# A decoder kernel: context spectra and keys moved into the first attention, correlation in two halves, accumulating transposes, a full last chunk

## The chip, the cores and the metric

The kernel runs on one core of one Trainium2 chip, as one program. The metric is its device time in microseconds (us). PE is the engine of matrix products (TensorE), DVE is VectorE, ACT is ScalarE, POOL is GpSimd, and SP (SyncE) issues the transfers. A chip core has on-chip memory (SBUF) and eight PSUM banks, into which PE writes.

## The reference, cut to what matters

A decoder of four layers; each layer adds an attention, a cross attention with a context and a feed-forward part to x, of 8 x 256 tokens and 256 features. Four parts matter here.

```python
# layer 0, attention: for each head h, q, k, v = 16x16 products of layernorm(x)
probs = softmax((q * k).sum(-1) / 16, axis=batch); x += probs * v.sum(over t)
# layer 0, cross attention: 16 heads of 16 features
q = layernorm(x) @ Wq.T + bq;  k, v = ctx @ Wk.T + bk, ctx @ Wv.T + bv
corr = irfft(rfft(q, t) * conj(rfft(k, t))).mean(head's features)
w, delays = top_k(corr, 5);  w = softmax(w)
x += (sum over delays of w * v shifted by delay) @ Wo.T + bo
# layer 0, feed-forward: mixture of 8 experts, two per token, 704 hidden features
y = (silu(z @ gate.T) * (z @ up.T)) @ down.T
# layer 3, attention: causal, with relative positions
att = q @ k.T + take_along(rel_pos_emb @ k.T, distance);  y = softmax(att / 4) @ v
```

## The kernel before, in words

Work is tiled in 16 tiles of 128 tokens (two a batch element), in four groups of four tiles for the norms. Each stage of the decoder is a class with one method per engine; the method writes that engine's instructions in their order, so each engine runs its own list, stage after stage, and waits only on counters (`wait_ge`). Nothing else orders the work. `Uses` deals out PSUM banks: `take` makes PE wait until the bank's last use has been emptied by the engine that was named for it, `fills` and `empties` raise the counters. All arithmetic that matters here is in float32. `products` (L218 to L222) is the helper that writes an accumulating product, so most of PE's records bear line 221; `copied` (L225 to L239) takes a bank out on ACT or DVE (L230, L234).

**Start (`begin`, L3336).** SP issues x, tables, the first stage's weights, the Fourier table and its inverse, and at the end two stores of zeros (2 MB each) for a result buffer of the second mixture (L3363). Norms of the four groups of x are begun by DVE (L253, L256), POOL (L263 to L271), z is written by DVE (L274: two tiles of a group) and ACT (L330: the other two), and PE turns z (L404), with copies out at L230 and L234.

**First attention (`L0Attention`, L616).** PE multiplies turned z by a 128x128 matrix, pair of tiles by pair (L651, eight pairs `qz`), and DVE multiplies the result with z (L681). Then DVE sums it by head over the 4096 columns (L684) and sums z over time (L687), takes a softmax across the batch (L693 to L698) and scales the values, which PE spreads over the partitions (L658, one bank for each of eight batch elements), adds them to x (L703, L706) and begins the next norm. SP waits for the logits (L694) and then issues the transfers of the next stage: the context (2 MB), four weights and four bias rows.

**Autocorrelation (`L0Autocorrelation`, L720).** PE, all by `spectrum` and `project`, eight banks each: spectra of the context, keys from them, spectra of z (waits for z), queries, values. DVE and ACT take the banks out in turns (`taken_out`), values go by ACT alone. POOL adds a bias to one row of each key, query and value (L923) and forms the fourth product of spectra (L935). DVE, when all queries and keys are in and biased, forms three products of 2048 columns (L872 to L874), sums over heads' features (L875, L876), subtracts (L878) and sums again (L879). PE inverts the result, a chain of short DVE operations picks the best five delays and weighs them (L885 to L900, ACT's exponential L850 in between), PE turns and transforms the weights, DVE and POOL multiply them with the values (L858), and PE inverts and projects. POOL's list has, between the values' biases and that, four additions of the output's bias to x (`Bias.pool`, L452, 1024 columns each).

**First mixture (`L0Mixture`, L1215).** 39 blocks of 128 rows, each with the weights of its expert (2.18 MB by SP from a ring of four). Per block PE does two halves of gate and up (352 columns), turns the 704 hidden features of the block before in six chunks of which the last has 64 (L1291), and multiplies them with `down` (six products of 256 columns, the last with 64 rows). ACT copies chunks 0 to 3 out (L1339), DVE the last two, each by a copy of its own (L1384); ACT takes out the block's result (L1348).

**Attention loop (`Attention`, L1666).** Used in the middle attention (layer 1, 48 units), in a smaller stage, and in the last one (layer 3, 48 units, with positions). A unit has two banks of scores: PE writes the mask (L1734), scores from 32-row tiles (L1738) and, with positions, adds them by products with the identity (L1743: eight blocks of 128x128 a unit); DVE takes the maximum (L1828), ACT the exponentials (L1803), PE turns them (L1754, eight transposes a unit), DVE copies (L1839), PE multiplies with the values (L1769) every other unit.

Of the kernel before, what the change touches and what calls it, by code (L numbers as in the profile page):

```python
# [13 lines left out]
ALU = mybir.AluOpType  # L14
# [3 lines left out]
P = 128  # L18
B, T, D = 8, 256, 256
TILES = B * T // P  # L20
DC = D // P
# [593 lines left out]

class L0Attention(Stage):  # L616


    def __init__(self, k):
# [4 lines left out]
        self.prod = k.slab[0].rearrange("p (i c) -> p i c", i=TILES)  # L624
        self.tmp = k.slab[1][:, 0:1024].rearrange("p (n a h e) -> p n a h e", n=2, a=2, h=H)
        self.fetch = Fetch(k, (self.wq, k.d["L0_attn_Wq"]), (self.wk, k.d["L0_attn_Wk"]), (self.wvT, k.d["L0_attn_WvT"]))
        self.norm = Norm(k)
        u = self.uses = Uses(k)
        self.m_use = u.add("dve")
        self.qz = [u.add("dve") for _ in range(TILES // 2)]  # L630
        self.v = [u.add("dve") for _ in range(B)]
# [6 lines left out]
    def pe(self):  # L638
# [5 lines left out]
        for n, u in enumerate(self.qz):  # L644
# [8 lines left out]
            mm.then_inc(use.fills(u), 1)  # L653
        pe.wait_ge(self.summed)
        for b, u in enumerate(self.v):
            bank = use.take(u)
            for c in range(DC):
                mm = nc.tensor.matmul(bank[:, P * c:P * c + P], self.sumT[:, B * c + b:B * c + b + 1].to_broadcast([P, P]),  # L658
                                      self.wvT, start=True, stop=True)
            mm.then_inc(use.fills(u), 1)  # L660
            if b % 2:
                self.next.norm.pe_final(b // 2)

    def act(self):
        act = self.k.act
        self.norm.act_zT(GROUPS - 1)
        act.wait_ge(self.shifted)
        self.k.nc.scalar.activation(self.s, self.s, ACT.Exp, scale=1.0 / float(D) ** 0.5).then_inc(self.exps.up(), 1)
        for g in range(GROUPS):
            self.next.norm.act_final(g)  # L670

    def dve(self):
# [26 lines left out]
        for b, u in enumerate(self.v):  # L699
            v4 = use.bank(u)[:, 0:D].rearrange("p (h e) -> p h e", h=H).unsqueeze(1).to_broadcast([P, 2, H, HD])  # L700
            p4 = self.s[:, 2 * b:2 * b + 2, :].unsqueeze(3).to_broadcast([P, 2, H, HD])
            dve.wait_ge(*use.filled(u))
            nc.vector.tensor_tensor(self.tmp[:, b % 2], v4, p4, ALU.mult).then_inc(use.empties(u), 1)  # L703
            dve.wait_ge(*use.emptied(u))
# [10 lines left out]
    def sp(self):  # L715
        self.k.sp.wait_ge(self.shifted)
        self.next.fetch.sp()


class L0Autocorrelation(Stage):  # L720


    def __init__(self, k):
        self.k, slab = k, k.slab
        self.ctx = slab[0].rearrange("p (i c) -> p i c", i=TILES)
        self.zfT, self.cfT = (slab[n].rearrange("p (c b f) -> p c b f", c=DC, b=B) for n in (1, 2))
        self.qf, self.kf, self.vf = (slab[n].rearrange("p (a b n) -> p a b n", a=2, b=B) for n in (3, 4, 5))
        self.wq, self.wk, self.wv, self.wo = (weight(slab[6], 512 * n, DC, D) for n in range(4))
# [12 lines left out]
        self.fetch = Fetch(k, (self.ctx, by_tile(d["ctx"])),  # L741
                           *[(w, by_chunk(d["L0_xattn_" + n])) for w, n in
                             ((self.wk, "WkT"), (self.wv, "WvT"), (self.wq, "WqT"), (self.wo, "WoT"))],
                           *[(r, d["L0_xattn_" + n]) for r, n in
                             ((self.bq, "bq"), (self.bk, "bk"), (self.bv, "bv"))],
                           (self.bo, d["L0_xattn_bo"].to_broadcast([P, D])))
# [4 lines left out]
        self.cf = [u.add(turns[b % 2]) for b in range(B)]  # L751
        self.kfs = [u.add(turns[(b + 1) % 2]) for b in range(B)]
        self.zf = [u.add(turns[b % 2]) for b in range(B)]
        self.qfs = [u.add(turns[(b + 1) % 2]) for b in range(B)]
# [6 lines left out]
        self.crossed = k.counter("cross_products", "pool").reserve(1)  # L761
# [7 lines left out]
    def spectrum(self, uses, src, ready):  # L769
        k, use = self.k, self.uses  # L770
        for b, u in enumerate(uses):
            for mark in ready(b):
                k.pe.wait_ge(*mark)
            bank = use.take(u)
            for c in range(DC):
                mm = products(k.nc, bank[:, T * c:T * c + T],
                              [(src[:, 2 * b + a, P * c:P * c + P], k.fourier[:, a, :]) for a in range(2)])
            mm.then_inc(use.fills(u), 1)

    def project(self, uses, src, w, spectra):  # L780
        k, use = self.k, self.uses
        for b, u in enumerate(uses):
            k.pe.wait_ge(*use.emptied(spectra[b]))
            bank = use.take(u)
            for half in range(2):
                mm = products(k.nc, bank[:, D * half:D * half + D],
                              [(src[:, c, b, P * half:P * half + P], w[:, c, :]) for c in range(DC)])
            mm.then_inc(use.fills(u), 1)

    def pe(self):  # L790
        k, nc, pe, use = self.k, self.k.nc, self.k.pe, self.uses
        pe.wait_ge(k.fourier_loaded)
        pe.wait_ge(self.fetch.loaded)
        self.spectrum(self.cf, self.ctx, lambda b: [])
        self.project(self.kfs, self.cfT, self.wk, self.cf)
        self.spectrum(self.zf, k.z, lambda b: self.norm.z_in(2 * b + 1))
        self.project(self.qfs, self.zfT, self.wq, self.zf)
        self.project(self.vfs, self.cfT, self.wv, self.cf)
# [25 lines left out]

    def spectra_out(self, engine, uses, dst, pattern, names):
        k, use = self.k, self.uses
        q = k.dve if engine == "dve" else k.act
        for b, u in enumerate(uses):
            if use.by(u, engine):
                q.wait_ge(*use.filled(u))  # L830
# [2677 lines left out]
```

## Time and profile before

| | |
|---|---|
| median of 3 runs | 2892.08 us (2885.71 to 2893.25) |
| profiled execution | 2892.69 us, span 2891.4 us |
| PE busy | 2459.8 us (85%) |
| DVE busy | 1218.3 us (42%) |
| ACT busy | 876.3 us (30%) |
| POOL busy | 556.1 us (19%) |
| mean granted clock of PE | 0.915 of 2.4 GHz |

Times in the profile are microseconds from the start of the span. A record names line, engine, operation, output from input by name, shape, and how many stand together; a matmul's record lasts longer than the step from one to the next, as they are pipelined, so a group is priced from its start to the next group's start. PEld are weight loads. In brackets stands the idle time before, and who ended it. Activity at which no engine waits for another is read from the groups' starts.

### The profile page before, as it was taken

What the parts mean: (1) busy time and instruction counts of PE and PEld (TensorE: products, weight loads), DVE (VectorE), ACT (ScalarE), POOL (GpSimd) and SP (SyncE); (2) the same over time, 40 slices, a digit from 0 to 9 for tenths busy, and PEclk for the clock granted to TensorE, in tenths of its full rate; (3) what the DMA queues carried; (4) which work ended last, traced back from release to release, by engine and by line L of the source; (5) the groups of instructions that cost most, each with busy time, mean ns of one, the idle gap of its engine ahead of it and who ended that gap; (6) DMA issues with size and microseconds to landing.
All of it is one profiled execution on the core that took longest, in us unless ns stands there. A gap on an engine that the chain in (4) does not pass through costs nothing.

```text
span 2891.4 us, 33874 instructions
## 1 busy us (share of the span) xinstructions
PE 2459.8 (85%) x13454; PEld 1668.8 (58%) x13454; DVE 1218.3 (42%) x2269; ACT 876.3 (30%) x2374; POOL 556.1 (19%) x552
## 2 busy tenths in 40 slices
PE   3965999949996779787999999699957999877999
PEld 3854666626674555223566657577732788633555
DVE  6363121257687472565333312300045455655220
ACT  1211222223673341563222321122214444313220
POOL 1441222224101011211444310233120100012000
PEclk8976999969898889898999998799977999988999
DMA  4004777730001000200000002233129232100000
GB/s 152 1 5 191 281 295 284 291 123 1 2 2 49 1 1 29 92 1 29 1 1 0 1 0 73 64 106 96 43 90 364 117 130 91 38 26 1 8 8 15
DMA packets 75380, 224.17 MB, mean 78 GB/s; under 512 B 9359, under 2 KB 52758, under 8 KB 65239
## 3 DMA queue, kind: packets, MB, share of 16 engines
q1 hardware_dynamic: 67894, 204.76, 19.5%
q0 software_dynamic: 7328, 17.26, 1.7%
q8 instruction: 106, 1.74, 0.2%
q14 instruction: 52, 0.42, 0.0%
HBM read 178.61 MB, written 45.17 MB: 77 GB/s over the span
## 4 chain that ended last, share of the span: by engine, by line
PE 48%; DVE 6%; DMA 2%; ACT 1%; POOL 1%; issue 1%; SPq 0%; POOLq 0%; DVEq 0%; ACTq 0%
PE psum L221 26%; PE psum L3198 6%; PE psum L1743 3%; PE psum L2241 2%; PE psum L3207 2%; PE psum L2228 2%; PE psum L1738 2%; DMA positions<-arena 2%; PE psum L1754 1%; DVE stats L253 1%; PE psum L1769 1%; DVE arena L2288 1%; PE psum L2458 1%; POOL small L2656 1%; PE psum L404 1%
## 5 line engine op out<-in xcount | busy, mean ns | idle before, releaser
L221 PE MATMUL psum<-arena 128*128 128x256 f32 (+6 forms) x4100 | 1060.6, 414 | 25.9 <-DVE arena L3294 12.9
L221 PEld LDWEIGHTS psum<-arena 128*128 128x128 f32 (+2 forms) x4100 | 717.3, 184 | 325.8 <-issue 160.5
L1828 DVE TENSOR_REDUCE small<-psum 128x4 f32<-128x1024 f32 (+1 forms) x112 | 137.0, 1223 | 157.4 <-PE psum L1743 110.9
L263 POOL TENSOR_SCALAR x_moments<-x_moments 128x4 f32<-128x4 f32 x48 | 12.0, 249 | 954.2 <-DVE x_moments L256 953.7
L3198 PE MATMUL psum<-arena 128*128 128x512 bf16 x768 | 166.4, 379 | 0.0
L1176 POOL DMA_INDIRECT l_out<-arena,slot_tables x79 | 78.7, 996 | 456.0 <-ACT arena L1348 255.5
L1803 ACT ACTIVATE arena<-psum,small 128x128 f32<-128x128 f32 (+1 forms) x384 | 148.9, 417 | 48.0 <-DVE small L1828 48.0
L1367 DVE TENSOR_TENSOR arena<-arena,psum 128x352 f32<-128x352 f32 x78 | 40.7, 521 | 265.5 <-ACT arena L1326 265.5
L1839 DVE COPY arena<-psum 128x512 f32<-128x512 f32 x224 | 143.6, 681 | 1.8 <-PE psum L1754 1.5
L1803 ACT ACTIVATE z<-psum,small 128x128 f32<-128x128 f32 (+1 forms) x256 | 103.8, 426 | 119.2 <-DVE small L1828 119.2
L404 PE MATMUL psum<-ident,z 128*128 128x128 f32 x256 | 47.1, 344 | 108.6 <-DVE z L274 79.9
L1738 PE MATMUL psum<-arena 32*128 32x128 f32 (+1 forms) x1280 | 133.2, 339 | 0.0
L3198 PEld LDWEIGHTS psum<-arena 128*128 128x128 bf16 x768 | 75.2, 98 | 90.5
L2656 POOL TENSOR_TENSOR small<-small,minus_half 128x16 f32<-128x16 f32 x32 | 92.8, 2901 | 179.2 <-DVE small L2570 179.2
L221 PE MATMUL psum<-zT,arena 128*128 128x512 f32 x240 | 115.2, 636 | 7.3 <-DVE zT L234 4.7
L2786 ACT ACTIVATE arena<-psum,small 128x269 f32<-128x269 f32 x128 | 61.5, 485 | 185.1 <-PE psum L221 173.6
L330 ACT ACTIVATE z<-x,x_shift,x_moments 128x256 f32<-128x256 f32 x96 | 52.2, 593 | 213.4 <-POOL x_shift L271 213.3
L1738 PEld LDWEIGHTS psum<-arena 32*128 32x128 f32 x1280 | 93.3, 191 | 38.9 <-issue 35.2
L221 PE MATMUL psum<-arena,zT 128*128 128x8 f32 (+2 forms) x384 | 108.7, 433 | 5.9 <-ACT zT L230 3.2
L404 PEld LDWEIGHTS psum<-ident,z 128*128 128x128 f32 x256 | 39.4, 181 | 118.4 <-DVE z L274 83.0
L1169 POOL DMA_INDIRECT arena<-z_rows,slot_tables x79 | 80.4, 1018 | 104.4 <-DVE slot_tables L1114 77.3
L1743 PE MATMUL psum<-ident,arena 128*128 128x128 f32 x768 | 100.2, 284 | 0.0
(334 smaller groups left out, 3464.3 us busy)
## 6 DMA issues: line engine op xcount, KB each, us to landing
arena<-L_ffn_w_in SPq DMA_DIRECT2D x39, 2176.0 KB, 8.8
arena<-L_ffn_W_in SPq DMA_DIRECT2D x16, 1024.0 KB
positions<-arena SPq DMA_DIRECT2D x16, 1024.0 KB, 6.0
arena<-positions SPq DMA_DIRECT2D x16, 1024.0 KB, 7.8
arena<-l_out SPq DMA_DIRECT2D x16, 512.0 KB, 8.1
positions<-arena SPq DMA_DIRECT2D x16, 512.0 KB, 6.6
arena<-positions SPq DMA_DIRECT2D x16, 512.0 KB, 8.7
l_out<-arena SPq DMA_DIRECT2D x2, 2048.0 KB, 14.0
```

The costliest lines, as they stand in the source:

```text
L221: last = nc.tensor.matmul(out, lhsT, rhs, start=(n == 0), stop=(n == len(pairs) - 1))
L404: t = nc.tensor.transpose(bank[:, P * j:P * j + P], src[:, P * c:P * c + P], k.ident)
L1169: k.nc.gpsimd.indirect_dma_start(out=out, out_offset=None, in_=k.z_rows[:, :], in_offset=bass.IndirectOffsetOnAxis(ap=self.router.token[0: ...
L1176: k.nc.gpsimd.indirect_dma_start(out=dram[:, :], out_offset=bass.IndirectOffsetOnAxis(ap=self.router.choice[0:count, n:n + 1], axis=0), in ...
L1738: mm = nc.tensor.matmul(bank[:, at:at + L], self.q[p][strip, c, P * t:P * t + P], self.kT[strip, c, P * keys[0]:P * keys[0] + L], start=Fa ...
L1743: mm = nc.tensor.matmul(bank[:, at + P * a:at + P * a + P], self.positions(t, a, head), k.ident, start=False, stop=True, skip_group_check= ...
L1803: e = nc.scalar.activation(buf[:, at:at + L], src[:, at:at + L], ACT.Exp, bias=self.minus_top(h)[:, i:i + 1], scale=1.0, accum_out=self.su ...
L1828: nc.vector.reduce_max(self.minus_top(h), use.bank(u).rearrange("p (h l) -> p h l", l=L), AX_X, negate=True).then_inc(self.topped.up(), 1)
L1839: nc.vector.tensor_copy(self.turned[h % 4][:, 512 * s:512 * s + 512], use.bank(u)).then_inc(use.empties(u), 1)
L2656: k.nc.gpsimd.tensor_tensor(inv, inv, k.minus_half, ALU.pow).then_inc(self.inverted.up(), 1)
L2786: nc.scalar.activation(self.hid[e % 2][:, m, span], use.bank(u)[:, 0:self.half], ACT.Gelu, bias=self.b1[:, e, m:m + 1]).then_inc(use.empti ...
L3198: mm = nc.tensor.matmul(bank, self.w1[:, c, P * m:P * m + P], p[:, c, :], start=(c == 0 and n == 0), stop=(c == MT - 1 and n == 2))
```

## The change

It has four parts.

1. Context. A new class `L0Context` shares the first attention's banks (now six). Its weights and the context are fetched in `begin`, ahead of the inverse table; the remaining weights of the autocorrelation right behind it, ahead of the zero stores. PE does one context spectrum after each of the eight `qz` pairs and the eight keys after the values; ACT takes out all of these, the spectra of a group behind the turned z of that group, and the keys ahead of its part of the next norm. The values of two batch elements share a bank. Scratch tiles moved to other slabs.
2. Correlation. The products, sums and subtraction are made for batch elements 0 to 3 and then 4 to 7, 1024 columns each, on POOL also. Queries 4 to 7 leave through ACT alone.
3. Positions are added with `is_transpose=True`.
4. The last chunk of the hidden features is 576 to 703 in place of 640 to 703; the `down` rows that would count features 576 to 639 twice are zero. DVE takes chunks 4 and 5 out by one copy.

```diff
@@ L0Context (new) @@
+        self.fetch = Fetch(k, (self.ctx, by_tile(d["ctx"])), (self.wk, by_chunk(d["L0_xattn_WkT"])), signal="context_loaded")
+    def add_spectrum(self):
+        self.cf.append(self.uses.add("act"))
+    def add_key(self):
+        self.kfs.append(self.uses.add("act", at=4 + len(self.kfs) % 4))
+    def pe_spectrum(self, b):
+        spectrum(self.k, self.uses, [(b, self.cf[b])], self.ctx, lambda b: [(self.fetch.loaded,), (self.k.fourier_loaded,)])
+    def pe_keys(self):
+        project(self.k, self.uses, enumerate(self.kfs), self.cfT, self.wk, lambda b: [self.uses.emptied(self.cf[b])])
@@ L0Attention.pe @@
             mm.then_inc(use.fills(u), 1)
+            self.context.pe_spectrum(n)
         pe.wait_ge(self.summed)
-        for b, u in enumerate(self.v):
+        for n, u in enumerate(self.v):
             bank = use.take(u)
...
+        self.context.pe_keys()
+        for g in range(GROUPS):
+            self.next.norm.pe_final(g)
@@ L0Attention.act @@
-        self.norm.act_zT(GROUPS - 1)
+        for g in range(GROUPS):
+            self.norm.act_zT(g)
+            spectra_out(k, "act", use, [(b, context.cf[b]) for b in (2 * g, 2 * g + 1)], context.cfT, DC)
         act.wait_ge(self.shifted)
...
+        spectra_out(k, "act", use, enumerate(context.kfs), context.kf, 2)
         for g in range(GROUPS):
             self.next.norm.act_final(g)
@@ L0Attention.sp @@
-        self.k.sp.wait_ge(self.shifted)
-        self.next.fetch.sp()
+        pass
@@ L0Autocorrelation @@
-        self.qfs = [u.add(turns[(b + 1) % 2]) for b in range(B)]
+        self.qfs = [u.add(turns[(b + 1) % 2] if b < B // 2 else "act") for b in range(B)]
...
+    def spectra_in(self, q, n):
+        for b in range(4 * n, 4 * n + 4):
+            q.wait_ge(*self.uses.emptied(self.qfs[b]))
+        q.wait_ge(*self.context.uses.emptied(self.context.kfs[-1]))
+        q.wait_ge(self.biased, B + 4 * n + 4)
+    def correlate(self, n):
+        nc, dve, at = self.k.nc, self.k.dve, slice(1024 * n, 1024 * n + 1024)
+        prod, summed, per_head = [p[:, at] for p in self.prod], self.summed[:, :, 64 * n:64 * n + 64], "p (r e) -> p r e"
+        (q0, q1), (k0, k1) = self.halves(self.qf, n), self.halves(self.kf, n)
+        self.spectra_in(dve, n)
         nc.vector.tensor_tensor(prod[0], q0, k0, ALU.mult)
...
@@ L0Autocorrelation.pool @@
-        self.pool_mean(self.kfs, self.kf, self.bk)
-        self.pool_mean(self.qfs, self.qf, self.bq)
...
+        self.pool_mean(self.context.uses, enumerate(self.context.kfs), self.kf, self.bk)
+        for n in range(2):
+            self.pool_mean(use, [(b, self.qfs[b]) for b in range(4 * n, 4 * n + 4)], self.qf, self.bq)
+            self.spectra_in(pool, n)
+            nc.gpsimd.tensor_tensor(self.prod[2][:, 1024 * n:1024 * n + 1024], self.halves(self.qf, n)[1],
+                                    self.halves(self.kf, n)[0], ALU.mult).then_inc(self.crossed.up(), 1)
+        self.pool_mean(use, enumerate(self.vfs), self.vf, self.bv)
         self.bias.pool()
@@ L0Mixture @@
-    def rows_of(self, m):
-        return min(P, self.I - P * m)
+    def features(self, m):
+        at = min(P * m, self.I - P)
+        return slice(at, at + P)
...
-                t = nc.tensor.transpose(bank[0:M, at:at + P], self.hid[j % 2][:, P * m:P * m + M], k.ident)
+                t = nc.tensor.transpose(bank[:, at:at + P], self.hid[j % 2][:, self.features(m)], k.ident)
...
-                for m in range(4, self.MT):
-                    M, at = self.rows_of(m), P * (m - 4)
-                    last = nc.vector.tensor_copy(self.hidT[(j - 1) % 2][0:M, m, :], use.bank(u)[0:M, at:at + P])
-                last.then_inc(use.empties(u), 1)
+                last = self.MT - 4
+                nc.vector.tensor_copy(self.hidT[(j - 1) % 2][:, 4:self.MT, :],
+                                      use.bank(u)[:, 0:P * last].rearrange("p (m t) -> p m t", m=last)).then_inc(use.empties(u), 1)
@@ Attention.pe_score @@
-                    mm = nc.tensor.matmul(bank[:, at + P * a:at + P * a + P], self.positions(t, a, head), k.ident, start=False,
+                    mm = nc.tensor.matmul(bank[:, at + P * a:at + P * a + P], self.positions(t, a, head), k.ident, is_transpose=True, start=False,
                                           stop=True, skip_group_check=True)
@@ begin @@
     nc.sync.dma_start(k.fourier[:, :, :], by_chunk(d["fourier"])).then_inc(k.fourier_loaded.up(), 16)
+    first.context.fetch.sp()
     nc.sync.dma_start(k.inverse[:, :, :], d["inverse"].rearrange("n p t -> p n t")).then_inc(k.fourier_loaded.up(), 16)
+    first.next.fetch.sp()
```

## Rows read from the trace of the kernel before

**Rows 1.** The page: shares of the chain that ended last, by engine.
```profile
PE 48%; DVE 6%; DMA 2%; ACT 1%; POOL 1%; issue 1%; SPq 0%; POOLq 0%; DVEq 0%; ACTq 0%
```
**Rows 2.** Timeline of PE, autocorrelation: start, duration, engine, line, operation, count.
```profile
68.98 16.32 PE L221 MATMUL psum<-fourier,arena 128*128 128x256 f32 x64 [14.09 <-DVE arena L703]
...
98.95 13.98 PE L221 MATMUL psum<-fourier,z 128*128 128x256 f32 x64
112.76 27.79 PE L221 MATMUL psum<-arena 128*128 128x256 f32 x128
```
**Rows 3.** Windows, PE: width, busy, granted clock, share and GB/s of transfers.
```profile
145.00:156.00 11.00, 0.12 (x1) 0.51 0.00 0
```
**Rows 4.** Timeline of PE in the last attention: one unit, and two later.
```profile
2335.15 2.05 PE L1743 MATMUL psum<-ident,arena 128*128 128x128 f32 x16
2337.04 1.04 PE L1754 MATMUL psum<-ident,z 128*128 128x128 f32 x8
2337.91 0.38 PE L1734 MATMUL psum<-causal 128*128 128x256 bf16 x2
...
2347.56 0.59 PE L1734 MATMUL psum<-causal 128*128 128x512 bf16 x2
```
**Rows 5.** Timeline of a block of the first mixture.
```profile
400.40 0.29 PEld L221 LDWEIGHTS psum<-arena 64*128 64x128 f32 x2 [0.33 <-issue]
401.14 0.37 ACT L1348 COPY arena<-psum 128x256 f32<-128x256 f32 x1 [2.54 <-PE psum L221]
...
404.16 2.53 PE L221 MATMUL psum<-arena 128*128 128x352 f32 x8
...
406.53 0.38 PE L1274 MATMUL psum<-ident,arena 128*128 128x128 f32 x2
...
409.73 0.37 ACT L1348 COPY arena<-psum 128x256 f32<-128x256 f32 x1 [2.54 <-PE psum L221]
```
**Rows 6.** Timeline of the first attention, all engines.
```profile
24.34 6.14 PE L651 MATMUL psum<-small,zT 128*128 128x128 f32 x32 [0.48 <-DVE small L675]
...
31.95 1.09 ACT L330 ACTIVATE z<-x,x_shift,x_moments 128x256 f32<-128x256 f32 x2
...
40.30 4.42 DVE L684 TENSOR_REDUCE small<-arena 128x256 f32<-128x4096 f32 x1
...
49.23 5.67 PE L658 MATMUL psum<-small 128*128 128x128 f32 x32 [9.70 <-DVE small L687]
...
73.30 0.23 POOL L271 TENSOR_SCALAR x_shift<-x_shift 128x4 f32<-128x4 f32 x1
```
**Rows 7.** Windows, PE, while the first transfers run (last figure: GB/s).
```profile
4.00:22.00 18.00, 3.88 (x16) 1.00 1.09 370
```
**Rows 8.** Timeline of the correlation, DVE, POOL and PE.
```profile
128.34 4.52 POOL L935 TENSOR_TENSOR z<-arena 128x2048 f32<-128x2048 f32 x1
128.39 6.61 DVE L872 TENSOR_TENSOR arena<-arena 128x2048 f32<-128x2048 f32 x1 [0.93 <-POOL arena L923]
...
144.43 11.28 POOL L452 TENSOR_TENSOR x<-x,arena 128x1024 f32<-128x1024 f32 x4
144.90 8.60 DVE L878 TENSOR_TENSOR z<-z 128x2048 f32<-128x2048 f32 x1
...
155.88 2.93 PE L221 MATMUL psum<-inverse,small 128*128 128x256 f32 x6 [15.33 <-DVE small L879]
...
163.94 0.35 DVE L900 TENSOR_SCALAR small<-small,arena 128x256 f32<-128x256 f32 x1
```
**Rows 9.** Timeline and windows (PE, PEld, DVE, ACT, POOL), middle attention; PE alone, early.
```profile
802.36 0.38 PE L1734 MATMUL psum<-causal 128*128 128x256 bf16 x2
...
808.35 0.38 PE L1734 MATMUL psum<-causal 128*128 128x256 bf16 x2
...
34.00:36.00 2.00, 0.57 (x5) 1.00 0.01 4
...
810.00:840.00 30.00, 30.00 (x378) 22.40 (x376) 26.11 (x39) 23.44 (x114) 0.00 (x0) 1.00 0.01 2
```

More of the change, by code:

```diff
@@ L724, in __init__ @@
         self.k, slab = k, k.slab
[L725 to L728, printed above, removed]
+        self.context = k.l0_context
+        self.zfT, self.cfT = slab[1].rearrange("p (c b f) -> p c b f", c=DC, b=B), self.context.cfT
+        self.qf, self.vf = (slab[n].rearrange("p (a b n) -> p a b n", a=2, b=B) for n in (3, 5))
+        self.kf = self.context.kf
+        self.wq, self.wv, self.wo = (weight(slab[6], 512 * n, DC, D) for n in range(1, 4))
         self.rows = slab[6][0:1, 2048:2048 + 3 * D]
@@ L767, in __init__ @@
         self.all_terms = k.counter("all_terms", "dve").reserve(B // 2)
[L769 to L788, printed above, removed]
     def pe(self):
         k, nc, pe, use = self.k, self.k.nc, self.k.pe, self.uses
-        pe.wait_ge(k.fourier_loaded)
         pe.wait_ge(self.fetch.loaded)
[L794 to L798, printed above, removed]
+        spectrum(k, use, enumerate(self.zf), k.z, lambda b: self.norm.z_in(2 * b + 1))
+        project(k, use, enumerate(self.qfs), self.zfT, self.wq, lambda b: [use.emptied(self.zf[b])])
+        project(k, use, enumerate(self.vfs), self.cfT, self.wv, lambda b: [])
         pe.wait_ge(self.correlated)
@@ L1298, in pe_out @@
         bank = use.take(self.y_use[j])
-        products(nc, bank[:, 0:D], [(self.hidT[j % 2][0:self.rows_of(m), m, :], self.down[j % self.RING][0:self.rows_of(m), m, :])
-                                    for m in range(self.MT)]).then_inc(use.fills(self.y_use[j]), 1)
+        products(nc, bank[:, 0:D], [(self.hidT[j % 2][:, m, :], self.down[j % self.RING][:, m, :]) for m in range(self.MT)]).then_inc(use.fills(self.y_use[j]), 1)
     def pe(self):
@@ L3379, in build @@
         stages = [s(k) for s in STAGES] + [Result(k)]
+        stages[0].next = stages[1]
         begin(k, stages[0])
@@ L3435, in layouts @@
     down = np.zeros((E, -(-I // P) * P, D), f)
-    down[:, :I] = a["L0_ffn_w_down"].transpose(0, 2, 1)
+    whole = I // P * P
+    down[:, :whole] = a["L0_ffn_w_down"].transpose(0, 2, 1)[:, :whole]
+    down[:, down.shape[1] - (I - whole):] = a["L0_ffn_w_down"].transpose(0, 2, 1)[:, whole:]
     o["L0_ffn_w"] = np.concatenate(
```

148 lines of the change are left out of this document (84 added, 64 removed).

## The prediction

> **What bounds the kernel now.** I read the page first. Of the chain that ended last, 48% is PE, and the shares of the other engines are small [rows 1]. So PE's instructions are worth money wherever PE's records stand back to back, and other engines' work only where PE waits for it. I then read the three stretches that the change touches, as timelines, and for each asked which wait ends last.
>
> In the autocorrelation PE has a front of 64 records each for context spectra, keys and z spectra, then 128 for queries and values, all back to back [rows 2]. After it PE stands nearly still for 11 us (0.12 us busy) while DVE and POOL form the correlation [rows 3]. In the last attention PE's groups follow each other without a gap [rows 4], and in the first mixture too, 8.59 us a block [rows 5]. So the first stage is bound by PE and then by DVE, the other two by PE.
>
> **Context moved (first attention).** Removed from the later stage: context spectra and keys, 30.0 us of PE from 68.98 until z spectra start at 98.95 [rows 2]. The last group's shift is written at 73.5 [rows 6], so z would be ready at about 74.7; 24 us of that PE time is on the path and would go if it could be hidden completely. It is not hidden completely. PE's order is now written as: one q·z pair, one spectrum, alternately, eight times.
> - Prices: a pair is 8 records of 128x128, at the full clock 0.118 each [rows 4], 0.93 us; the first 32 took 6.14 us, mostly at the lower clock [rows 6], so the first pair is 1.9. A spectrum is 8 records of 0.217 us (27.79 / 128, [rows 2]), 1.73 us warm; the first, at the lower clock, I take at 3.4 us (twice).
> - From 24.34 us: pairs and spectra 0 to 3 end at 37.3. Group 2 is turned and copied by 39.2. Pairs and spectra 4 and 5 end at 44.5. Then a new wait: ACT's queue now holds the copies of spectra 4 and 5 ahead of z of group 3, 1.09 us [rows 6], and PE waits for that z: turning begins at 46.5, pair 6 at 48.4, pair 7 ends at 52.0, its DVE product at 52.9. Behind ACT's waiting copy stands only that z; PE alone waits for it.
> - The two long DVE sums began at 40.30 and take 4.42 us each [rows 6]; now they begin at 52.9. The logits and values thus come **12.6 us later**: PE's products of the values start at 61.8 instead of 49.23.
> - Values take 5.5 us as before (they start cold again: PE idles 8 us), then the keys follow without a wait, 13.8 us, to 81.1. They lie beside DVE's additions and the norm, which on the same 12.6 us shift end with z of group 3 at 87.2. ACT takes out all keys before its z of groups 0 to 2 (three times 1.09 us, from 81.9): z spectrum 1 waits 0.2 us for that, the later ones nothing. So z spectra run from 81.1 to 95.2 against 98.95 to 112.8: **17.7 us earlier**, and the queries too: 109.0 against 126.6.
>
> Transfers: context and key weights (2.3 MB) now go ahead of the inverse table and of the zero stores, and the first spectrum waits for all three. Some 5.9 MB stand ahead; the queues moved 370 GB/s from 4 to 22 us [rows 7]; 5.9 MB at that rate are 16 us, which with the 4 us before lands them at 20, or at 24 if issue and landing add as much again. They are needed at 26.2, so this costs nothing; a transfer later than that would shift the stage one for one. The remaining weights follow at once, and the zero stores, some 9 us later, have no reader until the second mixture. SP's wait for the logits is gone.
>
> Moving two values into one bank removes four bank waits and adds one DVE step per pair; the next operation waited for that write anyway: 0.
>
> **Correlation in halves.** Before, DVE starts at 128.39 when the last query is out and biased, and ends with the sum before 155.88: 27.5 us [rows 8]. Uncontended, its parts are three products and a subtraction of 2048 columns, about 2.15 us each (6.61 less the rest of POOL's 4.52), and three sums of 2.3 (the last fits between 153.5 and 155.88): 15.5 us. The other 12 us are waits behind POOL: the first product took 6.61 us beside a POOL product of 4.52, and the subtraction 8.60 us beside the bias additions (11.28 for four) [rows 8]. Now half 0 starts once queries 0 to 3 are out and biased: 95.2 + 6.9 + 0.9 + 0.7 = 103.8. Half a POOL product (2.3) comes first, then three products of 1.1 with 0.7 us biases of POOL between them, two sums (1.15 each), subtraction, sum: about 12 us, to 115.8. Half 1 has its inputs long before; 9 us, to **124.8** (123 to 126). That is 31 us earlier than 155.8. The queries of half 1 all leave through ACT, 0.58 us each 1.73 us: it keeps up.
>
> Part of this is given back. The values leave PE at 122.9, so POOL's four bias additions now run from 124.1 to about 133.5, on top of the short DVE chain between the correlation and the weights (to 164.29 before, 5.5 us after its first copy, [rows 8]), which used to lie behind them. Upper bound of the cost: that the chain is held until the additions end, and begins only then, 9 us; lower bound 0, if no short operation waits. I take 5, near the upper half, since the one row with these very additions [rows 8] lost time. The Trainium skill ("SBUF — State Buffer", "SBUF: two separate sides") says the port pair that VectorE and GpSimd share is locked for a whole instruction, the loser blocking; 6.61 against 4.52 agrees with that. By that rule each of the chain's operations with a lock waits for one addition, and the chain ends when POOL does, at about 137.5. Sum for the stage: 31 − 5 = **26 us** (bounds 15 and 32: the former if halves lose more to POOL; what follows the weights is unchanged).
>
> **Accumulating transposes.** In the last attention each of 48 units adds its positions with 16 matmul records: from 2335.15 to the next group's start at 2337.04, 1.89 us, 0.118 each. The next eight records, true transposes of the same shape, run from 2337.04 to 2337.91: 0.109 each [rows 4]. A float32 matmul leaves two records, a transpose one, so 16 become 8: 0.87 us, and 0.06 us as my allowance for standing right behind the 32-row products. Saved: 1.89 − 0.93 = 0.96 us a unit. Is something else next? The middle attention is the same loop without positions: PE 30 of 30 us busy, DVE 26.11 and ACT 23.44, at the full clock [rows 9]. There a pair of units takes 5.99 us (808.35 − 802.36). In the last attention it takes 9.65 (2347.56 − 2337.91) and would take 7.7, so DVE and ACT, which have the same work in both, keep 1.7 us of slack a pair and PE stays the limit. 48 × 0.96 = **46 us** (bounds 41, if ends and fills swallow five units, and 48, for the cold ones). I price an accumulating transpose like a plain one; from below, no 128x128 record in the rows is cheaper than 0.109; from above it is the old 1.89 us, a gain of 0 (the second rival). Positions are fetched one batch ahead, six units, 29 us now and 23 then, against some 12 us of transfer: covered.
>
> The Trainium skill ("TensorE: Matmul & The Clock Gate", Terms) puts a float32 transpose at four times the speed of the multiplication; by that the sum would be 48 × (1.89 − 0.47) = 68 us. The rows say 0.109 against 2 × 0.118, and decide.
>
> **Full last chunk.** A block of the first mixture takes 8.59 us (409.73 − 401.14). Its parts: 16 records of 352 columns (2.37 / 8 = 0.296), 12 of 256 at 0.217, 8 transposes at 0.109: 8.21. The remaining 0.38 us lies around the two records with 64 rows, where weight loads stop 0.33 us before and after them [rows 5]. With all 128 rows that goes: 39 × 0.38 = **15 us** (bounds 10 and 16). Transposing 128 features instead of 64 costs nothing, as a 128-wide one takes the same 0.109. DVE saves a copy, hidden already by its idle time. Weight transfer, 2.18 MB a block at 8.2 us, is 266 GB/s, below the 370 of [rows 7].
>
> **Sum.** 26 + 46 + 15 = 87 us off. The profiled execution took 2892.69 us (span 2891.4 and 1.3 around it), the median of the runs is 2892.08. Forecast 2892.1 − 87 = **2805 us**. Its own range: all lower bounds give 66 (2826), all upper ones 96 (2796).
>
> **Rivals.**
> - *The first stage gives little.* The 12.6 us shift grows (a late context, ACT's queue) and POOL's additions block the chain fully. For: both waits are new. Against: PE stood idle for 9.7 us ahead of the values [rows 6]. Gain there 5: 2892 − 66 = 2826 and a little above, up to 2835. Chance 0.12.
> - *The change doesn't do what it says*: an accumulating transpose still takes two passes. Against: plain ones leave one record. 2892 − 41 = 2851. Chance 0.05.
> - *Slower: the clock.* With transposes in place of half of the products, PE could be granted the lower level in the last attention. That is 1.2 GHz in place of 2.4, granted for example from 146 to 156 us [rows 3]; I take every record at twice its time. A pair then takes 15.4 us in place of 9.65, 24 pairs 138 us more: 2892 − 41 + 138 = 2989. It makes the whole change a loss once some half of that stage runs so (24 × 7.7 = 185 us in all, against 87). Against: from 34 to 36 us PE was busy for 0.57 of 2 us and the level stayed at 1.00; so it did in the middle attention, where transposes are a third of PE's time [rows 9] (it would be half in the last). Chance 0.05. The Trainium skill ("TensorE: Matmul & The Clock Gate", Part 4: PE-mode transpose) says that the full clock does not engage for transposes, which don't count as busy in the same way; this is the rule that speaks against the change, and the trace shows no loss from it so far.
> - *More in the first stage*: no short operation waits for POOL, inside the forecast's range.
>
> **How the numbers follow.** The forecast has 0.78, of which some 0.05 falls outside its own range. Range 2794 to 2830: it takes in the likeliest and most of the first rival. A measurement tells about 0.3% (9 us) from no change. Faster 0.93, within 0.02, slower 0.05.
>
> **What the profile would show.** Right: spectra among the pairs from 26 us; L684's sum at 52.9; keys to 81; z spectra from 81; last correlation sum done at 125; POOL's additions beside DVE's short operations; L1743's successor with 384 records of which eight take 0.93 us; 8.2 us a block with no 64-row load. Wrong: PE waiting for the context at 26 us; a unit of the last attention whose next wait is DVE's maximum or ACT's exponential; a clock under 1.00 after 2280; a block still at 8.6 us.

## The result

| | before | changed |
|---|---|---|
| median | 2891.79 us | 2806.62 us |
| profiled execution, span | 2891.4 us | 2806.2 us |
| PE busy, records | 2459.8 us | 2396.2 us, x13070 |
| DVE busy | 1218.3 us | 1209.0 us |
| mean granted clock of PE | 0.915 | 0.915 |

The ratio of changed to before is 0.9709 (95% interval 0.9692 to 0.9725). Five more runs of the changed kernel, on another chip, gave 0.9710 (0.9697 to 0.9723). The predicted 2805 us was 1.6 us off, and the kernel is 85 us faster. PE lost 384 records, which is eight for each of the 48 units of the last attention.

### The profile page after: what moved, and what is told of

Its sections match the earlier page's. It is cut to its first block, busy times and chain, and to the rows that moved or that the text cites. A ratio compares the mean times of both kernels' runs of the same rounds, so it can differ in the third digit from the quotient of the medians.

```text
span 2806.2 us, 33074 instructions
## 1 busy us (share of the span) xinstructions
PE 2396.2 (85%) x13070; PEld 1626.3 (58%) x13070; DVE 1209.0 (43%) x2227; ACT 882.0 (31%) x2384; POOL 555.6 (20%) x553
## 3 DMA queue, kind: packets, MB, share of 16 engines
HBM read 178.61 MB, written 45.17 MB: 80 GB/s over the span
## 4 chain that ended last, share of the span: by engine, by line
PE 48%; DVE 7%; DMA 2%; ACT 1%; POOL 1%; issue 1%; SPq 0%; POOLq 0%; DVEq 0%; ACTq 0%
PE psum L221 27%; PE psum L3246 6%; PE psum L2289 2%; PE psum L3255 2%; PE psum L2276 2%; PE psum L1786 2%; PE psum L1791 2%; DMA positions<-arena 2%; PE psum L1802 1%; DVE stats L253 1%; PE psum L1817 1%; DVE arena L2336 1%; PE psum L2506 1%; POOL small L2704 1%; PE psum L404 1%
## 5 line engine op out<-in xcount | busy, mean ns | idle before, releaser
L221 PE MATMUL psum<-arena 128*128 128x256 f32 (+6 forms) x4100 | 1046.6, 413 | 26.3 <-DVE arena L3342 13.1
L1851 ACT ACTIVATE z<-psum,small 128x128 f32<-128x128 f32 (+1 forms) x256 | 103.8, 426 | 74.6 <-DVE small L1876 74.6
L221 PEld LDWEIGHTS psum<-arena,zT 128*128 128x128 f32 x384 | 72.2, 222 | 39.1 <-issue 28.1
```

Source lines behind the costliest of these rows:

```text
L221: last = nc.tensor.matmul(out, lhsT, rhs, start=(n == 0), stop=(n == len(pairs) - 1))
L1851: e = nc.scalar.activation(buf[:, at:at + L], src[:, at:at + L], ACT.Exp, bias=self.minus_top(h)[:, i:i + 1], scale=1.0, accum_out=self.su ...
```

## The profile after

PE's timeline in the first two stages (start, duration, engine, line, operation, count; the idle time before in brackets). L716 are the q·z pairs, L726 the values.

```profile
24.05 2.08 PE L716 MATMUL psum<-small,zT 128*128 128x128 f32 x8 [0.48 <-DVE small L747]
25.92 2.57 PE L221 MATMUL psum<-fourier,arena 128*128 128x256 f32 x8
28.32 1.05 PE L716 MATMUL psum<-small,zT 128*128 128x128 f32 x8
...
45.17 1.06 PE L404 MATMUL psum<-ident,z 128*128 128x128 f32 x8 [1.75 <-ACT z L330]
...
60.40 5.93 PE L726 MATMUL psum<-small 128*128 128x128 f32 x32 [7.96 <-DVE small L759]
66.17 13.98 PE L221 MATMUL psum<-arena 128*128 128x256 f32 x64
79.99 14.18 PE L221 MATMUL psum<-fourier,z 128*128 128x256 f32 x64
94.00 27.79 PE L221 MATMUL psum<-arena 128*128 128x256 f32 x128
124.77 1.56 PE L221 MATMUL psum<-inverse,small 128*128 128x256 f32 x6 [2.98 <-DVE small L919]
137.55 0.69 PE L855 MATMUL psum<-ident,small 128*128 128x128 f32 x2 [11.22 <-DVE small L950]
```

Against [rows 6] and [rows 2], the values start 11.2 us later (49.23 to 60.40). But the keys follow them at once, and the z spectra start 19.0 us earlier (98.95 to 79.99). The queries start 18.8 us earlier, and the inverse of the correlation 31.1 us earlier (155.88 to 124.77, [rows 8]). The last row carries the loss: PE waits 11.22 us for DVE's short chain, and turns the weights 26.8 us earlier than before (164.35 to 137.55). The timeline of DVE and POOL shows where the other 4 us stay.

```profile
102.67 2.36 POOL L983 TENSOR_TENSOR z<-arena 128x1024 f32<-128x1024 f32 x1
102.73 3.38 DVE L912 TENSOR_TENSOR arena<-arena 128x1024 f32<-128x1024 f32 x1 [0.93 <-POOL arena L973]
...
123.50 1.22 DVE L919 TENSOR_REDUCE small<-z 128x64 f32<-128x1024 f32 x1
124.00 9.23 POOL L452 TENSOR_TENSOR x<-x,arena 128x1024 f32<-128x1024 f32 x4
...
127.36 6.03 DVE L939 TENSOR_SCALAR small<-small,arena 128x256 f32<-128x256 f32 x1
```

L939 compares 256 columns. The next comparison of as many columns (L940) took 0.34 us; this one took 6.03, and ended at 133.39, just as POOL's four additions (124.00 + 9.23 = 133.23) did. It was issued during the second of them, so it waited through three. The copy and the maximum ahead of it had passed in 0.42 and 0.43 us beside the same additions.

A unit pair of the last attention, PE (L1791 adds the positions, L1802 turns the exponentials, L1782 starts the next unit):

```profile
2257.21 1.09 PE L1791 MATMUL psum<-ident,arena 128*128 128x128 f32 x8
2258.14 1.04 PE L1802 MATMUL psum<-ident,z 128*128 128x128 f32 x8
2259.01 0.38 PE L1782 MATMUL psum<-causal 128*128 128x256 bf16 x2
...
2266.74 0.59 PE L1782 MATMUL psum<-causal 128*128 128x512 bf16 x2
```

Where [rows 4] had 16 records and 1.89 us, there are 8 and 0.93 (2257.21 to 2258.14). A pair takes 7.73 us (2259.01 to 2266.74) in place of 9.65. The window over the same stage (width, busy time of PE, PEld, DVE, ACT, POOL, granted clock, share and GB/s of transfers) has the clock at its upper level, 2.4 GHz:

```profile
2300.00:2400.00 100.00, 100.00 (x1166) 80.38 (x1166) 68.25 (x103) 59.78 (x282) 0.00 (x0) 1.00 0.26 96
```

And ACT's timeline of the first mixture, two neighbouring blocks:

```profile
385.85 0.37 ACT L1397 COPY arena<-psum 128x256 f32<-128x256 f32 x1 [2.35 <-PE psum L221]
...
394.06 0.37 ACT L1397 COPY arena<-psum 128x256 f32<-128x256 f32 x1 [2.35 <-PE psum L221]
```

8.21 us a block, in place of 8.59 [rows 5]. Over all 39 blocks, from the first to the last such copy, 307.4 us (254.6 to 562.0) stand against 322.3 (280.8 to 603.1).

So the time went where the sum had it: 26.3 us up to the next stage (its first transfer starts at 169.75, before at 196.05), 14.9 in the mixture, and in the last attention 45.6 (scores from 2218.61 to 2405.16, before 2259.21 to 2490.37, which is 44.6, and 0.96 for the last unit). These make 86.8. The span has 85.2. The missing 1.6 us lie between and behind these stretches; a likely cause, not shown piece by piece, is that the clock falls and rises at other moments in each execution: from 870 to 890, for instance, this one was granted 0.59, and a second execution of the same kernel 0.82. The first stage moves by as much: in that second execution its end is at 171.75 and not at 169.75, which would be 24.3 us saved and not 26.3.

## Experiments

Times are given as ratios to the kernel before, on the same chip, since chips differ by some 7 us. One thousandth is 2.9 us.

### Each part alone

```diff
--- before.py   (transposes_only)
-  mm = nc.tensor.matmul(bank[...], self.positions(t, a, head), k.ident, start=False,
+  mm = nc.tensor.matmul(bank[...], self.positions(t, a, head), k.ident, is_transpose=True, start=False,
```

> The kernel before with one edit: positions are added with is_transpose=True. My theory: a unit's additions fall from 1.89 to 0.93 us, 48 units, 46 us off, so about 2846. Rival (the products take two passes in either form): eight records become no cheaper, 2892. Rival (lower clock): a pair of units at twice its time, some 138 us more than 2846.

Measured 0.9842 (0.9826 to 0.9859), 45.7 us of 2892. A unit's additions take 0.93 us here too (2291.07 to 2292.00).

The second kernel has part 4 of the change, with nothing else:

> The kernel before with the full last chunk alone (128 features from 576 on, with zero rows of down, and one copy on DVE). My theory: a block of the first mixture goes from 8.59 to 8.21 us, 39 times 0.38 = 15 us off, 2877. Rival: the 0.38 us is a cost of going between turning and multiplying, not of the 64 rows, and stays: 2892.

Measured 0.9953 (0.9937 to 0.9970), 13.6 us, with an interval of 9 to 18. The blocks say it more sharply: ACT's copies stand at

```profile
400.97 0.37 ACT L1349 COPY arena<-psum 128x256 f32<-128x256 f32 x1 [2.35 <-PE psum L221]
...
409.17 0.37 ACT L1349 COPY arena<-psum 128x256 f32<-128x256 f32 x1 [2.35 <-PE psum L221]
```

which is 8.20 us, and 307.4 over the 39 blocks. The 0.38 us was the price of the 64-row chunk, not of changing between turning and multiplying, which each block still does. The edit also merges DVE's two copies and turns 128 features in place of 64; neither was taken out by itself. But from 300 to 560 us no PE work of the kernel before waits for DVE, and the 60 pauses of the weight loads, 0.33 us each, that stood around the 64-row product are gone.

The third has parts 1 and 2:

> The changed kernel without its last two parts: the context and the keys in the first attention, and the correlation in halves. My theory: 26 us off, 2866, and with the other two single parts the savings add up to that of the whole change (85 us), as the three stretches share nothing. If they were to interact (the clock of PE, transfers), the sum would miss 85 by more than 3 us.

Measured 0.9911 (0.9895 to 0.9928), 25.7 us. The three savings add up to 85.0 us; the whole change has 84 (1 − 0.9710). Each of them is known to some 5 us only, so the parts don't interact by more than that shows.

### What the halves are worth, and what POOL takes

The undivided correlation, with the context still moved:

```diff
--- changed kernel   (context_whole_correlation)
-  for n in range(2):
-      self.correlate(n)              # 1024 columns
+  self.correlate()                   # 2048 columns, POOL's product too
...
```

> The changed kernel with the correlation undivided again (2048 columns at a time, on DVE and POOL). Theory (POOL's instructions hold DVE's): the subtraction meets POOL's additions of the bias, which begin at 124, and takes over 6 us; the chain of short operations ends at 142 to 145 in place of 137.5, so 5 to 8 us slower than the changed kernel, about 2813. Rival (what counts is only the columns after the last query): the correlation's last sum ends 5 us later and the short chain then takes its 10.8 us as well, 17 us later: 2823 or more. Second rival: the halves gain nothing, since the chain ends with POOL's additions in both forms, 2807.

Measured 0.9744 (0.9727 to 0.9760): some 10 us above the changed kernel. Its timeline:

```profile
126.16 11.28 POOL L452 TENSOR_TENSOR x<-x,arena 128x1024 f32<-128x1024 f32 x4
126.63 8.60 DVE L918 TENSOR_TENSOR z<-z 128x2048 f32<-128x2048 f32 x1
135.26 2.29 DVE L919 TENSOR_REDUCE small<-z 128x128 f32<-128x2048 f32 x1
...
146.08 0.69 PE L855 MATMUL psum<-ident,small 128*128 128x128 f32 x2 [5.54 <-DVE small L947]
```

The subtraction meets the additions and takes 8.60 us, as before the change [rows 8]. It doesn't wait for all four: it is through at 135.23, the additions at 137.44, and these take 11.28 us in place of 9.23. Asked for the additions alone (shortest, median and longest in ns), the kernel before shows the same:

```profile
L452 POOL TENSOR_TENSOR x<-x,arena x12: 2327/2342/4387, 144.4 to 2265.5; 128x1024 f32<-128x1024 f32 x12
```

The long one is the fourth (133.05 to 137.43 here, 151.32 to 155.71 before the change). So DVE waited through three additions, did its subtraction, and POOL's fourth waited for that. The weights are turned at 146.08 (8.5 us later, of which 0.6 were there at the z spectra already). I had put the end of the chain at 142 to 145; it is 146. The rival with 17 us and the one with none fall. Here the additions are over by the time of the short chain, which takes its own 5.54 us. So the additions cost DVE about 6 us in either form, once in the subtraction and once in the comparison, each through three additions.

If that is so, they should be moved to where DVE doesn't need what they hold:

```diff
--- changed kernel   (bias_early)
@@ L0Attention.pool @@
+  after.pool_rows()                          # factor on the bias rows
   for g in range(GROUPS):
       after.norm.pool_final(g)
+      if g < GROUPS - 1: after.pool_keys(g)  # biases of keys 2g, 2g+1
@@ L0Autocorrelation.pool @@
+  self.pool_keys(GROUPS - 1)
+  self.bias.pool()
...
   self.pool_mean(use, enumerate(self.vfs), self.vf, self.bv)
-  self.bias.pool()
```

> The changed kernel with POOL's work in another order: the factor on the bias rows and the keys' biases 0 to 5 in the first attention, and the four additions of the output's bias between the last norm and the queries' biases (from about 86), where POOL is idle, in place of behind the values' biases. Theory (the additions hold DVE's short operations): the one comparison that took 6.03 us takes its own 0.4, the short chain takes 5.5 us in place of 10.8, and the kernel is 5.3 us faster than the changed one. Rival (the 6 us have another cause, such as the exponential on ACT): no change. Counter-effect: DVE's copies of z spectra beside the additions wait up to 2.3 us each; with six banks PE shouldn't notice.

```profile
88.36 9.28 POOL L452 TENSOR_TENSOR x<-x,arena 128x1024 f32<-128x1024 f32 x4 [0.24 <-DVE z L274]
90.69 0.69 DVE L234 COPY arena<-psum 128x512 f32<-128x512 f32 x1 [1.21 <-PE psum L221]
...
129.01 0.34 DVE L943 TENSOR_SCALAR small<-small,arena 128x256 f32<-128x256 f32 x1
...
133.52 0.69 PE L859 MATMUL psum<-ident,small 128*128 128x128 f32 x2 [5.54 <-DVE small L954]
```

The comparison takes 0.34 us and PE waits 5.54 in place of 11.22. From the first z spectrum to the turned weights there are 51.9 us (81.65 to 133.52), against 57.6 (79.99 to 137.55): 5.7 us gone, 5.3 were expected. (The second execution of the changed kernel has 57.5, from 81.69 to 139.23.) The whole time gives 0.9691 (0.9676 to 0.9706), 5 us less than the changed kernel, with overlapping intervals. The counter-effect I had feared isn't there: DVE's copies out of PSUM keep their 0.69 us beside the additions, and the additions their 9.28.

Both edits together, the undivided correlation with the additions moved:

> The undivided correlation, with POOL's additions moved ahead of the queries' biases. Theory (the additions held the subtraction): it takes about 2.8 us in place of 8.60, the comparison in the short chain 0.35, and the weights are turned at about 139.5, where the halves with the additions moved had 133.5: so the halves are worth some 6 us by themselves. Rival (it was the long instructions of 2048 columns that made DVE slow, not the additions): the subtraction still takes over 6 us.

```profile
127.28 2.28 DVE L922 TENSOR_TENSOR z<-z 128x2048 f32<-128x2048 f32 x1
...
140.40 0.69 PE L859 MATMUL psum<-ident,small 128*128 128x128 f32 x2 [5.54 <-DVE small L951]
```

The subtraction takes 2.28 us, so the 8.60 came from the additions and not from its 2048 columns. From the z spectra (81.22) there are 59.2 us, 7.3 more than with halves: the halves are worth 7 us by themselves. The ratio, from two runs, is 0.9720 (0.9702 to 0.9738), 8 us above that of the halves with the additions moved.

### A later wait moved up

PE waits 8 us for the sum of z over time, which DVE makes second of two long sums.

```diff
--- changed kernel   (sum_first)
+  reduce_sum(self.sumT ..., k.zT ...)     # moved ahead
   dve.wait_ge(*use.emptied(self.qz[-1]))
   dve.step(reduce_sum(self.s, self.prod ...))
-  reduce_sum(self.sumT ..., k.zT ...)
```

> The changed kernel with DVE's two long sums (4.42 us each) in the other order, so that the sum of z over time, for which PE waits with its values, comes first. If PE is what sets the end from the values to the correlation, everything up to the weights comes up to 4.4 us earlier. Rival (the norm's z is next: its last group is ready at 86 whatever PE does): less than 2 us, since z spectra 6 and 7 then wait for z.

The values start at 55.72, 4.7 us earlier, but the weights are turned at 133.80, 3.75 earlier. Most of the difference is the clock: the 32 records of the values take 6.57 us (55.72 to 62.29) against 5.77. PE's windows (width, busy PE, PEld, DVE, ACT, POOL, granted clock):

```profile
54.00:56.00 2.00, 0.28 (x1) 0.28 (x2) 2.00 (x2) 0.00 (x0) 0.00 (x0) 0.75 0.00 0
56.00:58.00 2.00, 2.00 (x10) 2.00 (x10) 2.00 (x1) 0.00 (x0) 0.00 (x0) 0.50 0.00 0
58.00:60.00 2.00, 2.00 (x12) 2.00 (x11) 1.99 (x1) 0.00 (x0) 0.00 (x0) 0.50 0.00 0
60.00:62.00 2.00, 2.00 (x12) 2.00 (x12) 1.46 (x3) 0.42 (x1) 0.00 (x0) 0.54 0.00 0
```

The idle gap is only 3.38 us long, yet the level falls to 1.2 GHz all the same, some 0.7 us before PE begins again, and stays there until about 61.8. How long it stays low isn't fixed by the gap. The values' rows of this run, of the next one, which has the same gap, and of the second execution of the changed kernel:

```profile
55.72 6.74 PE L726 MATMUL psum<-small 128*128 128x128 f32 x32 [3.38 <-DVE small L757]
...
55.92 5.33 PE L726 MATMUL psum<-small 128*128 128x128 f32 x32 [3.38 <-DVE small L757]
...
61.53 6.51 PE L726 MATMUL psum<-small 128*128 128x128 f32 x32 [7.96 <-DVE small L759]
```

To the start of the keys these are 6.57, 5.17 and 6.34 us, and the last is the kernel that took 5.77 in its first execution. So a single profile can be off by 1 us here, and the 0.8 us isn't a price of this edit: against the second execution the weights come 5.4 us earlier. Whole: 0.9699 (0.9685 to 0.9714).

> Both edits: POOL's work in the other order, and the sum of z over time first. Theory: 5.3 + 4.4 = 9.7 us faster than the changed kernel, if the queries' biases, which POOL starts behind its additions at 95, are still in time for the first half of the correlation (needed at 98.3); if not, 2 to 3 us of it are lost.

Measured 0.9687 (0.9674 to 0.9701), against 0.9710 (0.9697 to 0.9723) for the changed kernel in as many runs: 6.6 us less, and by the two intervals between 1 and 12. The weights are turned at 129.22, 8.3 us earlier than in the changed kernel's profile. By rows that is 4.5 for the earlier sum, 0.6 for values that happened to run faster, and 5.7 for the additions, less 2.5: from the first z spectrum to the first query there are 16.5 us (74.90 to 91.37) in place of 14.0. There the z of the last groups is next. The earlier sum makes PE ready for it sooner, and the keys' biases stand between POOL's parts of the norms: DVE begins the third group's z at 83.06, in the run with the sum alone at 82.28. I had allowed for a loss of 2 to 3 us, but by late biases of the queries.

```profile
74.90 7.50 PE L221 MATMUL psum<-fourier,z 128*128 128x256 f32 x32
...
83.82 3.72 PE L221 MATMUL psum<-fourier,z 128*128 128x256 f32 x16 [1.43 <-DVE z L274]
```

This is the lowest ratio measured. The repeated changed kernel:

> The changed kernel once more, unedited, for a comparison of ratios with the two edits that moved POOL's work and the sum: 0.971 of the kernel before, as in its first runs, between 0.9695 and 0.972. If it is at 0.969, the two edits together gained nothing in the whole.

It came to 0.9710, so the two edits together did gain.

### Do transposes keep the clock

```diff
--- changed kernel   (gap_of_transposes; gap_of_products has 28 plain products here)
+  for _ in range(60):
+      nc.tensor.transpose(spare, k.ident, k.ident)
   pe.wait_ge(self.summed)
```

> The changed kernel with 60 more 128x128 float32 transposes of the identity, into a bank that nobody reads, in the 8 us in which PE waits for the sum of z over time (from 52.4). The question is the clock: the products of the values behind that gap are 32 records in 5.8 us, where warm ones take 3.8. If transposes keep the granted clock at its upper level, the filling takes 6.5 us, the gap's rows show 1.00, and the values take 3.8 us. Rival (the Trainium skill, TensorE: Matmul & The Clock Gate, Part 4: transposes don't engage the full clock): the values still take 5.8 us, as behind an idle gap.

> The same with 28 plain 128x128 float32 products (56 records of 0.118, 6.6 us) in place of the 60 transposes. Products should keep the clock, so the values take 3.8 us here by either theory; it is the comparison for the run with transposes. If even this leaves the values at 5.8 us, the pair says nothing on transposes.

With transposes:

```profile
52.30 6.71 PE L722 MATMUL psum<-ident 128*128 128x128 f32 x60
60.42 3.84 PE L729 MATMUL psum<-small 128*128 128x128 f32 x32 [1.41 <-DVE small L762]
64.10 13.98 PE L221 MATMUL psum<-arena 128*128 128x256 f32 x64
```

and its windows:

```profile
56.00:58.00 2.00, 2.00 (x21) 2.00 (x20) 2.00 (x1) 0.00 (x0) 0.00 (x0) 1.00 0.04 8
...
60.00:62.00 2.00, 1.58 (x14) 1.58 (x15) 1.48 (x4) 0.42 (x1) 0.00 (x0) 1.00 0.00 0
```

With products:

```profile
53.62 6.41 PE L722 MATMUL psum<-ident 128*128 128x128 f32 x56
61.74 3.84 PE L729 MATMUL psum<-small 128*128 128x128 f32 x32 [1.71 <-DVE small L762]
```

The values take 3.68 us (60.42 to 64.10, and 61.74 to 65.42) with either filling, against 5.77 and 6.34 behind the idle gap in the two executions of the changed kernel. Each filling was run once. Sixty transposes, with no product among them for 6.7 us, kept the upper level as products did. The Trainium skill ("TensorE: Matmul & The Clock Gate", Part 4: PE-mode transpose) says that the full clock does not engage for transposes; these rows don't agree, at least for keeping a level that PE already has. Whether transposes alone would raise it wasn't tried. By the way, the filling brings the z spectra from 79.99 to 77.91.

### How much DVE has to spare in the last attention

```diff
--- changed kernel   (extra_maximum)
   def dve_max(self, h):
...
+      if self.positions is not None and h % 2:
+          dve.step(nc.vector.reduce_max(...))    # the same maximum once more
       nc.vector.reduce_max(...).then_inc(self.topped.up(), 1)
```

> The changed kernel with one more maximum of 1024 columns (1.22 us) on DVE in every second unit of the last attention, written to the same place. Theory: DVE and ACT have 1.7 us to spare in a pair of units, so it costs nothing (under 3 us over the stage). Rival (since the transposes became cheap, DVE's maximum is on PE's path): 24 times 1.2 = 29 us slower.

Measured 0.9744 (0.9729 to 0.9759), about 10 us slower: neither the nothing that I expected nor 29. The rows:

```profile
2347.75 1.23 DVE L1877 TENSOR_REDUCE small<-psum 128x4 f32<-128x1024 f32 x1 [1.61 <-PE psum L1791]
...
2349.01 1.23 DVE L1878 TENSOR_REDUCE small<-psum 128x4 f32<-128x1024 f32 x1
...
2350.15 1.28 DVE L1889 COPY arena<-psum 128x512 f32<-128x512 f32 x2
...
2350.88 0.42 PEld L1802 LDWEIGHTS psum<-ident,z 128*128 128x128 f32 x4 [0.23 <-DVE arena L1889]
2350.88 1.25 PE L1802 MATMUL psum<-ident,z 128*128 128x128 f32 x8
```

The transposes take 1.25 us in place of 1.04, and what they wait for is DVE. They turn exponentials that ACT had finished by 2347; but they write the two banks that DVE empties by its copies (L1889), and these copies now stand behind two maxima. From 2240 to 2380 us the transposes' weight loads wait for that copy 29 times, 5.7 us in total; the changed kernel has no such wait in that stretch. From one unit's mask to the next's, the longer unit of a pair takes 4.93 us in place of 4.56 in two pairs of three, and 4.66 in place of 4.52 in the third. So of the 1.22 us added to a pair 0.85 to 1.1 were absorbed and 0.29 on average seen, 7 us over 24 pairs; the other 3 of the 10 us are within the interval.

## Why the prediction was right

- **Context moved: right.** I had the values 12.6 us later; they are 11.2. Of the difference 1.0 is the first spectrum, which I took cold at 3.4 us: it took 2.40 here (25.92 to 28.32). That isn't a wrong price: in the second execution of the same kernel it took 3.41 (25.88 to 29.29), and in the other runs between 1.7 and 3.4. It is a matter of when the clock rises, as the pace of the records suggests; the granted clock reads 1.00 there in both executions and doesn't settle it. The new wait for ACT's z is there at 45.17, 1.75 us. From the values on, every step lies 1.1 to 1.4 us before the forecast one (60.40, 79.99 and 94.00 against 61.8, 81.1 and 95.2); in the second execution they are 61.53, 81.69 and 95.71. No row has PE waiting for the context or its weights, so their earlier transfers cost nothing.
- **Correlation in halves: right.** Half 0 began at 102.73 (forecast 103.8) and took 12.7 us (12); the end is 124.77 (124.8). That the numbers met is luck: an earlier start by 1.1 and longer halves by 1; in the second execution the end is 126.45.
- **What POOL gives back: cause right, the size partly by luck, the detail not.** I took 5 us; with the additions PE waits 11.22 us, without them 5.54, so they cost 5.7. The upper bound of 9 us was mis-sized: it counts from the first addition, but the chain begins behind the inverse, at 126.37, and could be held for 6.9 us at most, to 133.23. (The inverse ahead of the chain, at the full clock now, took 1.4 us less than in [rows 8], which is why only 4.3 of the 31.1 us were given back; my sum had no such term.) The Trainium skill ("SBUF — State Buffer", "SBUF: two separate sides") led me to expect that each short operation with a lock waits for one addition, with a chain that ends when POOL does. The rows don't agree: one operation waited through three additions, several before it didn't wait at all, and the others ran behind, so that the chain ended at 137.50, 4.3 us after POOL. The forecast named 133.5 for POOL and 137.5 for the chain in two places, which by its own rule can't both be; the second number was right for another reason.
- **Accumulating transposes: right.** 0.93 us as priced, 45.6 to 45.7 us against 46. The price of a plain transpose held for an accumulating one. The Trainium skill's four times ("TensorE: Matmul & The Clock Gate", Terms) would have given 68; the rows say 1.89 to 0.93, twice.
- **Full last chunk: right.** 8.21 us a block, 14.9 us against 15.
- **The slack: wrong, without harm.** I read 1.7 us a pair for DVE and ACT out of the middle attention's period. Added at one place, 1.22 us were not free. A difference of periods is a sum over a loop; the slack of the one path from DVE's second maximum over its copy of turned scores to the bank of PE's next transposes was 0.85 to 1.1 us. The forecast didn't hang on it: the changed kernel doesn't wait there inside the loop.
- **The rivals.** The first stage gave its full gain; eight records less a unit rule out two passes; the lower clock did not come, and the pair with filled gaps shows no loss from transposes to a level that PE already has.

What stays open: why the copies and the maximum pass beside POOL's additions while the comparison doesn't, beyond that the former read PSUM or are reductions; why DVE's turn came after three additions both times; and what moves the moments at which the clock falls between two executions of one kernel, which is 2 to 3 us of each comparison.

## What to carry to other kernels

Price a change per loop from the start of one group to the next, and check the same step in each single part: three stretches that share no engine time add up. An engine pair that blocks each other should be planned like one resource: look at which short chain a long POOL operation falls upon after the change, and move it to where DVE only copies out of PSUM. Before counting on slack in a loop, ask which single path has it, and read who releases the wait rather than who stands next to it. Before explaining 1 us in a profile by an edit, look at the same rows in a second execution of the same kernel.

## What the runs showed of the hardware

- A DVE comparison of 256 columns (0.34 us alone) beside POOL additions of 2.3 us each waited through three of them, 6.03 us with its own time. A DVE subtraction (2.28 us alone) also waited through three, 8.60 us, and then ran ahead of the fourth, which took 4.39 us. Copies from PSUM (0.69 us), the maximum of eight (0.43) and sums over features (1.21) ran beside POOL's work at their own times.
- 60 transposes in a row (6.7 us) kept the clock at 2.4 GHz like products, and the 32 records behind them took 3.68 us. Behind an idle gap of 3.38 us, which ended in 1.2 GHz, the same records took 6.57 and 5.17 us in two executions, behind one of 7.96 us 5.77 and 6.34.
- One product with 64 of 128 rows (two records) in a block of the mixture came with 0.38 us a block beyond its own time, in pauses of the weight loads of 0.33 us before and behind it; with all 128 rows, zeros among them, these were gone.
